# A graph-attention layer on one core: sources under their own semaphore, histogram mask and row field on Pool, accumulator cleared by ScalarE

## What is computed

```python
def head(w1, bb1, w2, bb2, a1, aab1, a2, aab2):
    feats = jnp.maximum(x @ w1 + bb1, 0.0) @ w2 + bb2          # 256 -> 256 -> 64
    x_cat = jnp.concatenate([feats[row], feats[col], elem[:, None]], axis=1)
    hid = jnp.maximum(x_cat @ a1 + aab1, 0.0)
    e1 = jax.nn.leaky_relu((hid @ a2 + aab2)[:, 0], negative_slope=0.2)
    w = jnp.exp(e1 - jnp.max(e1))
    pooled = jax.ops.segment_sum(w[:, None] * feats[col], row, num_segments=n)
    return pooled / (jax.ops.segment_sum(w, row, num_segments=n) + 1e-10)[:, None]
# row = src, col = dst, elem = edge_weight
# out = layernorm(x + the four heads side by side)
```

## Time and profile before

| | |
|---|---|
| Median of 3 timed runs | 5230.21 us (5229.04 to 5233.76) |
| The profiled execution | 5190.44 us, its span 5188.7 us |
| PE busy | 4402.2 us (85%) |
| PEld busy | 3093.9 us (60%) |
| DVE busy | 4550.7 us (88%) |
| ACT busy | 3761.1 us (72%) |
| POOL busy | 2702.7 us (52%) |
| Mean granted clock of PE | 0.956 |
| HBM traffic | 850.50 MB, 164 GB/s over the span |

### The profile page before, as it was taken

How to read it: one execution, slowest core, us unless ns; L and a number is a source line. 1 busy time by engine, 2 the same in 40 slices (tenths; PEclk the granted TensorE clock), 3 DMA queues, 4 the chain that set the end, 5 groups by cost and what they waited for, 6 DMA issues and landing times.

```text
span 5188.7 us, 133139 instructions
## 1 busy us (share of the span) xinstructions
PE 4402.2 (85%) x24914; PEld 3093.9 (60%) x24915; DVE 4550.7 (88%) x25629; ACT 3761.1 (72%) x12720; POOL 2702.7 (52%) x2834
## 2 busy tenths in 40 slices
PE   1499899999986899999999999999999999999920
PEld 0255555555554666767677767767677767767610
DVE  7799999999998789888899889889898889898853
ACT  0467766766762688888888888888888888888832
POOL 1266666666666555555555555555555555555522
PEclk9799999999997999999999999999999999999965
DMA  2032333333333777777777777777777777777623
GB/s 79 23 73 67 78 72 71 75 74 72 69 78 93 227 216 218 218 219 217 216 218 217 217 218 219 217 218 216 217 218 216 219 215 219 215 220 216 200 87 117
DMA packets 287022, 850.50 MB, mean 164 GB/s; under 512 B 98946, under 2 KB 138114, under 8 KB 286966
## 3 DMA queue, kind: packets, MB, share of 16 engines
q0 software_dynamic: 169920, 673.54, 46.8%
q1 hardware_dynamic: 74638, 160.14, 9.7%
q10 hardware_dynamic: 42408, 16.21, 1.2%
HBM read 738.46 MB, written 111.26 MB: 164 GB/s over the span
## 4 chain that ended last, share of the span: by engine, by line
PE 29%; ACT 25%; DVE 6%; issue 4%; DMA 4%; DVEq 1%; POOL 0%; ACTq 0%; POOLq 0%; SPq 0%
ACT z L1092 17%; PE psum L949 12%; PE psum L953 7%; PE psum L936 6%; DVE z L1503 3%; ACT onehot L1121 3%; DMA out_dram<-z 3%; ACT onehot_t L1110 3%; PE psum L962 2%; ACT onehot L1125 2%; PE psum L973 1%; DVE z L1493 1%; PE psum L921 1%; DVE acc L1552 1%; DVEq L1552 0%
## 5 line engine op out<-in xcount | busy, mean ns | idle before, releaser
L734 POOL DMA_INDIRECT z<-qf_table,rec x1664 | 1593.6, 958 | 1567.0 <-PE psum L936 1035.8
L1092 ACT ACTIVATE z<-z 128x64 f32<-128x64 f32 x6656 | 1651.5, 336 | 56.6 <-ACT z L1099 56.3
L949 PE MATMUL psum<-p_win,onehot_t 128*128 x9984 | 1434.0, 276 | 207.7 <-ACT onehot_t L1110 90.5
L949 PEld LDWEIGHTS psum<-p_win,onehot_t 128*128 128x128 bf16 x9984 | 963.9, 97 | 777.8 <-issue 460.6
L936 PE MATMUL psum<-z,onehot 128*128 128x260 f32 x3328 | 1027.2, 391 | 2.8 <-DVE acc L1552 1.9
L953 PE MATMUL psum<-z,ident 128*128 128x258 f32 x3328 | 1004.0, 383 | 0.0
L1503 DVE SCALAR_TENSOR_TENSOR z<-z,a_b 128x129 f32<-128x129 f32 x3328 | 893.0, 292 | 0.0
L1503 DVE SCALAR_TENSOR_TENSOR z<-psum,a_b 128x129 f32<-128x129 f32 x3328 | 822.6, 283 | 0.0
L1552 DVE TENSOR_TENSOR acc<-acc,psum 125x260 f32 x1664 | 698.7, 420 | 78.6 <-PE psum L936 48.8
L1493 DVE TENSOR_TENSOR z<-z,psum 128x258 f32<-128x258 f32 x1664 | 691.9, 416 | 39.4 <-PE psum L953 29.6
L666 POOL DMA_INDIRECT sorted_rows<-z x300 | 483.3, 1611 | 406.9 <-DVE z L1384 162.4
(11 more groups left out here) (221 smaller groups left out, 6363.0 us busy)
## 6 DMA issues: line engine op xcount, KB each, us to landing
p_table<-acc SPq DMA_DIRECT2D x100, 377.9 KB
p_win<-p_table SPq DMA_DIRECT2D x100, 377.9 KB
qf_table<-acc SPq DMA_DIRECT2D x75, 378.9 KB
z<-qf_table,rec POOLq DMA_INDIRECT x1664, 4.6
acc<-in_x_dram SPq DMA_DIRECT2D x25, 500.0 KB
z<-in_x_dram SPq DMA_DIRECT2D x20, 625.0 KB
out_dram<-z ACTq DMA_DIRECT2D x20, 625.0 KB
qf_table<-z SPq DMA_DIRECT2D x25, 378.9 KB
```

What stands on the lines that cost most here:

```text
L734: pool.indirect_dma_start(out=z_t[:, o + j, :], out_offset=None, in_=qf_table, in_offset=bass.IndirectOffsetOnAxis(ap=rec[:, o + j, 3:4].b ...
L949: mm = pe.matmul(to, onehot_t[:, j, :], p_flat[:, bass.ds((w % 2) * (3 * ZW) + (part * ZW + o), n)], start=(part == 0), stop=(part == 2 an ...
L1092: op = act.activation(z_t[:, slot, o:o + DO], z_t[:, slot, o:o + DO], ACT.Copy, scale=z_t[:, slot, o + DO:o + HF])
```

## The change

- `src` is counted by a semaphore of its own, `s_src`; DVE starts with it. `s_edges` counts the other two loads, and is waited for where the weights and destinations are first used.
- The step that writes row + 1 into `fields` moves from DVE to POOL, which waits for DVE's seventh step. POOL builds `same_col` before it, and waits for the weights behind it. DVE waits for the row field (`s_row_field`) ahead of the first one-hot, whose histogram overwrites `edge_t`.
- DVE's digits use another buffer, so that high and low digit follow each other without a wait.
- A histogram step takes its result in three: ACT copies the PSUM block to `hist_m`, POOL multiplies it there by `same_col`, DVE reduces it. DVE reduces a step two steps later than its one-hot (before: one step later for odd steps, in the same for even ones).
- POOL no longer clears the accumulator. ACT does it in 13 pieces of 2000 columns, one behind each of its field copies, and takes over the waits. It reads a column of zeros, `zero_col`.

```diff
-        N_EDGE = 17
+        N_EDGE = 16
...
-            sp.dma_start(src_i[0:EP, :], src.rearrange("(p c) -> p c", p=EP)).then_inc(s_edges, 16)
+            sp.dma_start(src_i[0:EP, :], src.rearrange("(p c) -> p c", p=EP)).then_inc(s_src, 16)
...
+            pool.memset(zero_col[:, :], 0.0).then_inc(s_const, 1)
...
-            pool.wait_ge(s_weights, N_W)
-            pool.tensor_copy(ad_q[:, 0, HALF:HALF + P], ident[:, :]).then_inc(s_const, 1)
-            pool.tensor_copy(ad_q[:, 1, HALF:HALF + P], ident[:, :]).then_inc(s_const, 1)
-
             pool.affine_select(out=same_col, in_=ones_f[:, 0:HCOL * LO].rearrange("p (c n) -> p c n", c=HCOL), pattern=[[-HI, HCOL], [0, LO]],
...
-            pool.wait_ge(s_edges, 48)
+            pool.wait_ge(s_edge_step, 7)
+            pool.tensor_scalar(fields[0:EP, :, 0], edge_t[0:EP, :], 1.0, None, ALU.add).then_inc(s_row_field, 1)
+
+            pool.wait_ge(s_weights, N_W)
+            pool.tensor_copy(ad_q[:, 0, HALF:HALF + P], ident[:, :]).then_inc(s_const, 1)
+            pool.tensor_copy(ad_q[:, 1, HALF:HALF + P], ident[:, :]).then_inc(s_const, 1)
+
+            pool.wait_ge(s_masks, 2)
+
+            def hist_mask(n, b):
+
+                pool.wait_ge(s_hist_out, n + 1)
+                pool.tensor_tensor(hist_m[:, b, :, :, :], hist_m[:, b, :, :, :], same_col.unsqueeze(1).to_broadcast([P, HG, HCOL, LO]), ALU.mult).then_inc(s_hist_mask, 1)
+
+            def count_windows(g):
+                for b in range(2):
+                    hist_mask(g * 2 + b, b)
+
+            loop(pool, N_HIST // 2, count_windows)
+
+            pool.wait_ge(s_edges, 32)
...
-            pool.wait_ge(s_ends, 2)
...
-            pool.memset(acc[:, :], 0.0).then_inc(s_acc_zero, 1)
...
-            pe.wait_ge(s_const, 18)
+            pe.wait_ge(s_const, 19)
...
-                    since(pe, s_hist_mask, n - 1)
+                    since(pe, s_hist_out, n - 1)
...
+            def hist_out(n, b):
+
+                act.wait_ge(s_hist, n + 1)
+                since(act, s_hist_ev, n - 1)
+                act.activation(hist_m[:, b, :, :, :].rearrange("p m c n -> p (m c n)"), psum[:, b, 0:HG * HCOL * LO], ACT.Copy).then_inc(s_hist_out, 1)
...
+            part = acc.shape[1] // BULK
             for g in range(BULK):
                 act.wait_ge(s_field_mm, g + 1)
                 act.activation(rec_all[:, g * P:(g + 1) * P, 1:3].bitcast(BF16)[:, :, 0:3],
                                psum[:, g % 2 * 6 + 1, 0:3 * P].rearrange("p (f t) -> p t f", f=3), ACT.Copy).then_inc(s_field_b, 1)
+                act.activation(acc[:, g * part:(g + 1) * part], zero_col[:, :].to_broadcast([P, part]), ACT.Copy).then_inc(s_acc_zero, 1)
...
-            dve.wait_ge(s_edges, 48)
+            dve.wait_ge(s_src, 16)
...
-            dve.tensor_scalar(fields[0:EP, :, 0], ta, 1.0, None, ALU.add).then_inc(s_edge_step, 1)
             dve.tensor_copy(ui, edge_win[0:EP, :]).then_inc(s_edge_step, 1)
-            dve.wait_ge(s_edge_step, 9)
-            dve.tensor_scalar(ti, ui, LO.bit_length() - 1, None, ALU.logical_shift_right).then_inc(s_edge_step, 1)
+            dve.wait_ge(s_edge_step, 8)
+            dve.tensor_scalar(ra.bitcast(I32), ui, LO.bit_length() - 1, None, ALU.logical_shift_right).then_inc(s_edge_step, 1)
+            dve.tensor_scalar(ui, ui, LO - 1, None, ALU.bitwise_and).then_inc(s_edge_step, 1)
             dve.wait_ge(s_edge_step, 10)
...
+            dve.wait_ge(s_const, 17)
+            dve.wait_ge(s_masks, 2)
             dve.wait_ge(s_edge_step, 12)
...
+            dve.wait_ge(s_row_field, 1)
...
-                dve.wait_ge(s_hist, n + 1)
-                dve.tensor_tensor(hist_m[:, b, :, :, :], psum[:, b, 0:HG * HCOL * LO].rearrange("p (m c n) -> p m c n", m=HG, c=HCOL),
-                                  same_col.unsqueeze(1).to_broadcast([P, HG, HCOL, LO]), ALU.mult).then_inc(s_hist_mask, 1)
                 dve.wait_ge(s_hist_mask, n + 1)
...
-                hist_onehot(g, 0)
-                if not isinstance(g, int) or g:
-                    hist_take(g * 2 - 1, 1)
-                hist_onehot(g, 1)
-                hist_take(g * 2, 0)
+                for b in range(2):
+                    hist_onehot(g, b)
+                    if not isinstance(g, int) or g:
+                        hist_take(g * 2 + b - 2, b)
...
+            dve.wait_ge(s_edges, 32)
...
-            dve.wait_ge(s_acc_zero, 2)
+            dve.wait_ge(s_acc_zero, 1 + BULK)
```

48 lines of the change are left out of this document (27 added, 21 removed).

## The result

| | kernel before | changed kernel |
|---|---|---|
| Timed median, first timing | 5230.30 us (5229.04 to 5233.76, 4 runs) | 5169.67 us (5166.48 to 5170.16, 4 runs) |
| The profiled execution, its span | 5190.44 us, 5188.7 us | 5166.48 us, 5164.7 us |
| Mean granted clock of PE | 0.956 | 0.963 |

The ratio is 0.9882, 95% interval 0.9865 to 0.9899: 60.6 us faster, where 44.7 were forecast.

What follows compares the result with a forecast made beforehand. Bound: three stretches where one engine works and others wait (start, histogram, the 60 us before the edge loop). Gains 28.6 + 1.3 + 14.8 = 44.7 us, taken from 5230.2, gave 5185.5 us; range 5175 to 5211.

Steps and rivals of the forecast that it cites:

- the sorting loop: Stretch from 0.2 to 1.6 ms, before the edge loop; the diff touches nothing in it, so no gain was counted.
- Start: Up to the first histogram matmul: sources in at 10 us, PE starting at about 35.5 instead of 42.29, behind the weights.
- Not more than 7 us: Start: the sources' own semaphore is worth at most some 7 us, since the weights are what is late next.
- Histogram step: Histogram loop: mask moved to POOL, period 1.6 us instead of 2.04; 28.6 us gained, some 7 of it the start.
- Rivals 1 and 2: Histogram: mask stops DVE between compares every step, 5207.6 us, chance 0.22; or alternating, about 1.8 a step, 5194.9 us, 0.20.
- rival 1: Histogram: POOL's mask gets in between the two compares, 2.07 us a step, gain 22.6, 5207.6 us; chance 0.22.
- Rival 3: Histogram: POOL's mask is dear, 1.1 us or more; 1.6 between the compares would give 5254.6 us; chance 0.06.
- rival 4: Start: the sources come no earlier despite their own semaphore, 10 us lost, 5195.5 us; chance 0.03.
- rival 5: Behind the sorting loop: ACT's clearing takes 3 us a piece, period 3.7, 12 us lost, 5198 us; chance 0.03.
- Table load: ACT's only table load before the edge loop, at 192.35 us, moves into idle time in the histogram: 1.3 us gained.
- Clearing: Between sorting and edge loop: DVE's shift falls from 22.82 to 0.52 us, ACT clears behind field copies: 14.8 us gained.
- The reference: Whole kernel: timed median 5230.2 lies 0.8% above the profiled 5190.4; the same gain was subtracted from it.

Runs made afterwards that it cites:

- second timing: The changed kernel timed again with no edit, beside the kernel before at 5189.2 us: 5134.3 us, ratio 0.9896, a gain of 54.9 us.

## Why the prediction was wrong

Most mechanisms came as forecast. Two terms were mis-sized: the time that POOL's mask needs the port, and the sorting loop, which was put at nothing. A third error is one of reference. The first alone does not leave the range, whose low end allowed for a histogram step of 1.47 (5179.4 us).

- **Start: right.** Forecast: sources at 10, seven steps to 19.6, PE at 35.5 behind weights and copies. Measured 10.3, 20.0, 35.09. The row field was put at 5.5 us and took 8.78; it cost nothing, as the row field moved back to VectorE showed. "Not more than 7 us" is 7.2.
- **Histogram step: the first term that failed.** The forecast counted the port as 0.94 for the compares plus 0.6 for the mask, 1.54, and took 1.6. Measured is 1.46, DVE's own work. The step that was wrong is that the mask needs the port for its whole duration: twice the mask added 0.45 us of waiting and half a mask 0.23. 0.94 + 0.45 = 1.39 is below DVE's 1.46, so nothing is left over. Over 47 steps 1.6 against 1.463 is 6.4 us: histogram and start gave 35.1 instead of 28.6. The 0.6 for the mask's duration was right (0.64), as was the place: forecast was a request 1.20 us behind the end of a pair, 0.07 inside the narrow compare; measured 1.16 to 1.18 and 0.03 to 0.06.
- **The place was in part luck.** The forecast let ACT's copy wait for PE's matmuls and "for nothing else". The kernel also lets it wait until DVE has reduced the block that was in the buffer, and in about every second step this is what ends last ([1.06 <-DVE z L1255] at 62.60 above). Reduction and matmuls end within 0.1 us of each other, so the number came out all the same.
- The Trainium skill (SBUF — State Buffer, section "SBUF: two separate sides") says that whoever starts first holds the shared pair for the whole instruction. The order agrees with both experiments; "the whole instruction" does not agree in length: 0.45 of 0.64 us. The Trainium skill's statement (same page, section "Who interferes with whom") that a reduction never contends agrees with the mask that ends under it at no cost.
- **A row that was overlooked.** The prediction says that no reduction stands beside POOL in the trace of before. In the edge loop some do, also beside a POOL product:

```profile
1735.67 0.24 POOL L719 TENSOR_TENSOR bias_mask<-ab_b,rec 128x32 f32<-128x32 f32 x1
...
1735.74 0.21 DVE L1525 TENSOR_REDUCE tile_max<-e_val 128x4 f32<-128x32 f32 x1
```

Neither is held up: the 208 reductions of this line take 0.204 to 0.218 us, and 0.245 is the shortest of the 208 products. So the trace of before could have shown that a mask may be hidden under a reduction.

- **Rivals 1 and 2** did not come, but rival 1 is real: it came in one step of 50, and the mask in halves, which asks 0.08 us earlier than the whole mask, makes it in nearly every step. Its price was too high, though: by 0.45 per mask a whole mask between the compares gives 1.91, not 2.07. **Rival 3** (a mask of 1.1 us or more), **rival 4** (sources late; 12.6 us when they were made late, forecast 10) and **rival 5** did not come. The chances of all that is faster by more than 0.2% add up to 0.92, not 0.91.
- **Table load: right**, 1.3 us: ACT's first instruction of the sorting loop comes 36.4 us earlier, the last reduction 35.1; the load now stands at 0.78 us.
- **Clearing: right.** Forecast 14.8; the way from the last scatter to the last field copy is 15.2 us shorter in the first pair of traces, and the part alone gave 15.6 in time. The clearing was put at 2.02 us by ACT's wider forms, which made ACT the bound by 0.04 us (2.72 against 2.68 a group); it took 1.85, and PE stayed the bound at 2.66. The estimate of 1.85 for 2000 columns that follows from the figures of the Trainium skill (ScalarE: Activation LUTs, section "What ACT_TABLE_LOAD costs") agrees with these rows; by it PE would be the bound, as it was.
- **The sorting loop: the second term that failed.** The prediction put it at nothing, since the diff touches nothing in it. From the first instruction of it to the last scatter the changed kernel was 5 us shorter (36.4 earlier at its begin, 41.5 at its end). DVE's picks in it span 1408.7 and 1409.2 us in the two traces of before, 1404.5, 1403.9 and 1405.5 in the three of the changed kernel, and 1404.4 to 1409.4 in those of the nine edited kernels. Two of these nine (gathers spaced out, each piece cleared twice) differ from the changed kernel only behind the sorting loop and take 1406.9 and 1407.1; the row field on VectorE takes 1408.5 and is as fast in time as the changed kernel. So the loop's length moves by up to 5 us with no part of the change that I could name, and whether the change shortened it at all is not shown. This is open, and a range for this kernel should have had these 5 us in it.
- **The reference.** "0.8% above, for which the trace gives no reason": the same program takes 5189 us in two timings and 5230 to 5236 in two others, and the profiled execution is of the first kind, the timed runs are of the second (on which chips those two were taken is not on record). I treated the difference as the same for both kernels. "The edge loop otherwise of the same length" holds between traces of the first kind (3260 us before, 3255 changed) and not between unlike ones (3294).

Together: 44.7 + 6.5 (histogram) + 0.4 (clearing) + up to 5 (sorting loop) = 56.6, against 56.8 at the edge loop's start and 54.9 in time on the chip where before takes 5189. The parts add in time too: 31.6 (histogram alone) + 15.6 (clearing alone) + 7.2 (the start, by the traces) = 54.4. The other 5.7 us of the first timing's 60.6 are within its interval, 53 to 71 us. They also decide about the range: with the 54.9 of the second timing the 44.7 would have been missed all the same, but 5230.2 - 54.9 = 5175.3 lies just inside it.

## What to carry to other kernels

In this histogram, where VectorE is the bound of a short loop, moving one of its products to an idle engine was worth the whole product, because the mover's request falls behind the last VectorE instruction that needs the shared port and a reduction follows. In a loop of this kind look for the order inside one step, in hundredths of a microsecond; splitting the moved work into smaller pieces brought the request too early here. A long POOL instruction can hold a VectorE one for nearly its whole length (8.66 us beside 8.78), so it belongs where something else is late anyway, or on ScalarE (0.99 for the same VectorE shift). And before a trace is set against a timing, see that both say the same of the same program; here they differed by 40 us.

## What I had not expected of the hardware

- The same program takes 5189 us on two chips and 5229 to 5237 in the two other timings, with the runs of one kernel in one timing within 13 us. Where it is longer, VectorE waits 24 to 28 us in 11 to 15 places for a releaser that the trace doesn't see (four traces; none of the nine traces from the two faster timings and the first profiled execution has such a wait in this line), the longest ones (up to 11.5 us) at the first gathers of the edge loop, while the DMA engines move 300 GB/s.
- ScalarE's activation over 125x1600 elements into every sixth bf16 value takes 5.65 us, 3.5 ns a column, where its dense clearing of 2000 f32 columns takes 1.85. POOL's same step took 8.78 beside VectorE, VectorE's 2.83.
- A POOL product of 256 columns lasts 0.64 us but keeps VectorE from its next two-input instruction for 0.45.
